# Attention over 23104 keys: four score banks, scores in a row, and maximum jobs on a ring of three PSUM banks

## The reference

```python
# x: (16, 100, 256), ctx: (16, 1444, 256); H = 16 heads of 16
def xattn(x, cond):                       # x is layer-normalised before
    q = (x @ Wq + bq) * hd ** -0.5        # all 1600 queries see all 23104 keys
    k, v = split(cond @ Wkv + bkv)
    q, k = fq_sym(q, axis=-1), fq_sym(k, axis=-1)      # to 8 bits and back, per row and head
    v = fq_sym(v, axis=2)                              # per column, over all keys
    attn = softmax(q @ k.T)                            # per head
    attn = fq_unsigned(attn, axis=-1)     # steps of max(attn) / 255 along the keys
    return (attn @ v) @ Wp + bp
x = x + xattn(layernorm(x), ctx)
x = x + ffn(layernorm(x))                 # 8 experts, two of them weighted, low-rank corrections
```

## Time and profile before

| | us |
|---|---|
| median of 3 runs | 8433.32 (8431.86 to 8435.04) |
| the profiled execution | 8431.64 |
| its span in the trace | 8429.8 |
| granted TensorE clock, mean | 0.976 |
| busy: PE, DVE, ACT, POOL | 8040.4, 6627.4, 5391.9, 5189.8 |
| the reductions of the jobs, L1316 | 5686.0 in 5017 |
| the exponentials, L1202 | 4978.3 in 11520 |

### The profile page before, as it was taken

How to read it: one execution, slowest core, us unless ns; L and a number is a source line. 1 busy time by engine, 2 the same in 40 slices (tenths; PEclk the granted TensorE clock), 3 DMA queues, 4 the chain that set the end, 5 groups by cost and what they waited for, 6 DMA issues and landing times. The chain is left out here.

```text
span 8429.8 us, 176589 instructions
## 1 busy us (share of the span) xinstructions
PE 8040.4 (95%) x60394; PEld 2517.5 (30%) x60394; DVE 6627.4 (79%) x6516; ACT 5391.9 (64%) x12186; POOL 5189.8 (62%) x3571
## 2 busy tenths in 40 slices
PE   7957999999999999999999999999999999999688
PEld 4512222222222222222222222222222222222343
DVE  8985888888888888888888888888888888884566
ACT  2314777777777777777777777777777777777333
POOL 5765666666666666666666666666666666666356
PEclk9968999999999999999999999999999999999789
DMA  5663020202020201111110202020202020110000
GB/s 162 209 215 87 25 37 23 39 19 43 18 44 14 46 16 39 23 38 23 32 30 25 38 25 37 23 39 19 43 18 44 14 47 16 39 21 22 9 4 4
DMA packets 305513, 351.63 MB, mean 42 GB/s; under 512 B 66003, under 2 KB 286879, under 8 KB 295903
## 3 DMA queue, kind: packets, MB, share of 16 engines
q1 hardware_dynamic: 304788, 342.27, 17.5%
q10 hardware_dynamic: 42, 0.00, 0.0%
HBM read 263.57 MB, written 78.41 MB: 41 GB/s over the span
## 5 line engine op out<-in xcount | busy, mean ns | idle before, releaser
L1316 DVE TENSOR_REDUCE mpart<-psum 128x1 f32<-128x978 f32 (+1 forms) x5017 | 5686.0, 1172 | 1300.4 <-PE psum L1444 1202.0
L1202 ACT ACTIVATE y<-psum 128x400 f32<-128x400 f32 x11520 | 4978.3, 506 | 2013.1 <-PE psum L1532 2001.7
L1119 POOL TENSOR_SCALAR xh<-y 128x1600 f16<-128x1600 f32 x2880 | 4397.8, 1527 | 2699.7 <-PE psum L1512 1775.0
L1532 PE MATMUL psum<-QT,K 99*128 99x400 bf16 x11520 | 3107.3, 339 | 50.5 <-ACT y L1202 48.9
L1502 PE MATMUL psum<-y,ones 128*17 128x400 f32 x23040 | 2526.6, 505 | 0.0
L1532 PEld LDWEIGHTS psum<-QT,K 99*128 99x128 bf16 x11520 | 834.5, 97 | 2491.5 <-ACT y L1202 1972.2
L1444 PE MATMUL psum<-K,QS 48*128 48x489 bf16 x8334 | 1440.4, 379 | 88.0 <-DVE mpart L1316 34.4
L1512 PE MATMUL psum<-xh,vwin 128*16 128x400 f16 x11520 | 1015.5, 334 | 12.0 <-DMA vwin<-v_int 11.3
L1444 PEld LDWEIGHTS psum<-K,QS 48*128 48x128 bf16 x8334 | 362.7, 93 | 1038.6 <-issue 860.1
L1502 PEld LDWEIGHTS psum<-y,ones 128*17 128x17 f32 x23040 | 401.4, 95 | 723.0 <-issue 722.5
L1512 PEld LDWEIGHTS psum<-xh,vwin 128*16 128x16 f16 x11520 | 321.1, 90 | 631.4 <-issue 488.9
(11 more groups left out here) (187 smaller groups left out, 2490.1 us busy)
## 6 DMA issues: line engine op xcount, KB each, us to landing
K<-kT_parts SPq DMA_DIRECT2D x288, 240.0 KB, 8.4
vwin<-v_int SPq DMA_DIRECT2D x579, 80.0 KB, 1.9
K1X<-kT_parts SPq DMA_DIRECT2D x760, 45.8 KB
kT_parts<-part SPq DMA_DIRECT2D x135, 256.0 KB, 2.8
src<-in_ctx_dram SPq DMA_DIRECT2D x46, 512.0 KB, 4.2
v_float<-kv SPq DMA_DIRECT2D x45, 512.0 KB, 4.7
vin<-v_float SPq DMA_DIRECT2D x9, 2560.0 KB, 15.3
K<-kT_parts SPq DMA_DIRECT2D x32, 450.9 KB
```

The lines of the kernel that those rows point to most:

```text
L1119: pool.tensor_scalar(xh[:, g % YR, :, :], y[:, g % YR, :, :], INT_STEP, 0.0, ALU.mult, ALU.add)\
L1202: act.activation(y[:, s % YR, j, :], s2_bank(tiles_before(h, b, c) + GT * s + j), ACT.Exp).then_inc(exp_done, 1)
L1316: dve.tensor_reduce(mpart[:, t, column], buf[:, :, 0:CHALF], AX.XY, ALU.max).then_inc(s1_free, 1)
L1532: pe.matmul(s2_bank(T + t), K3[0:MROW, c * REGION + t * P:c * REGION + (t + 1) * P], queries, start=True, stop=True).then_inc(s2_ready, 1)
```

## The change

The eight PSUM banks are divided anew: three (0 to 2) for maximum jobs and four (3 to 6) for scores; ACC stays bank 7. Slots now count banks, not jobs: slot n lies in bank n % 3, and a job takes two slots. Each of its two matmuls raises s1_ready by one; the job waits until both of its banks are free (s1_free >= at + n + 2, with 3 given at the start). VectorE reduces each bank by itself into its own column of mpart, which has 48 columns a tile in place of 24. `maxima` and `turn_out` take three slots in place of two. SPLIT and LATE are gone: all four scores of a group are issued in a row, and then all of its jobs. JOBS_AT is as before, and so is the order of sums and values. SyncE's thresholds are rewritten in the new count.

```diff
-S2_RING = 3
+S2_RING = 4
+S1_RING = 3
-SPLIT = ((1, 4, 8, 12, 14), (1, 4, 8, 12, 14), (2, 5, 9, 14))
-LATE = ((), (), (12,))
-SLOT_AT = (0, N_JOBS[0] + 2, N_JOBS[0] + 2 + N_JOBS[1])
-SLOTS_BLOCK = sum(N_JOBS) + 4
-PRO_SLOTS = 4 * CHUNKS + 2 + LEAD
+SLOT_AT = (0, 2 * N_JOBS[0] + S1_RING, 2 * N_JOBS[0] + S1_RING + 2 * N_JOBS[1])
+SLOTS_BLOCK = 2 * sum(N_JOBS) + 2 * S1_RING
+FIRST_MAX = 8 * CHUNKS
+PRO_SLOTS = FIRST_MAX + S1_RING + 2 * LEAD
-            mpart = sb("mpart", [P, PT + 1, CHUNKS], F32)
+            mpart = sb("mpart", [P, PT + 1, 2 * CHUNKS], F32)
-        def s1_buf(n):
-            return psum[:, 2 * (n % 2):2 * (n % 2) + 2, :]
+        def s1_bank(n):
+            return psum[:, n % S1_RING, :]
-            return psum[:, 4 + j % S2_RING, 0:QB]
+            return psum[:, S1_RING + j % S2_RING, 0:QB]
...
-            after_job(4 * CHUNKS - 1)
+            after_job(FIRST_MAX - 1)
...
                 act.wait_ge(mt_copied, turn + 1)
-                act.sem_inc(s1_free, 2)
+                act.sem_inc(s1_free, S1_RING)
...
         @block.vector
-            def job(t, column, at, n, buf):
-
-                dve.wait_ge(s1_ready, at + n + 1)
-                dve.tensor_reduce(mpart[:, t, column], buf[:, :, 0:CHALF], AX.XY, ALU.max).then_inc(s1_free, 1)
+            def job(t, chunk, at, n, bank):
+
+                for k in range(2):
+                    dve.wait_ge(s1_ready, at + n + k + 1)
+                    dve.tensor_reduce(mpart[:, t, ds(2 * chunk + k, 1)], bank(n + k)[:, 0:CHALF], AX.X, ALU.max)\
+                        .then_inc(s1_free, 1)
...
         @block.tensor
-            def job(tile, keys, at, n, buf):
-
-                pe.wait_ge(s1_free, at + n + 1)
+            def job(tile, keys, at, n, bank):
+
+                pe.wait_ge(s1_free, at + n + 2)
                 for k in range(2):
                     top, end = HALVES[k]
-                    last = pe.matmul(buf[:, k, 0:CHALF], tile[top:end, :], keys[top:end, :], start=True, stop=True)
-                last.then_inc(s1_ready, 1)
+                    pe.matmul(bank(n + k)[:, 0:CHALF], tile[top:end, :], keys[top:end, :], start=True, stop=True)\
+                        .then_inc(s1_ready, 1)
...
                     if c == BODY_C - 1 and s == TURN_AT and B < LASTB:
-                        maxima(B + 1, at, done, job_buf(c, done))
-                        extra = 2
-                    score_tile(s, 0)
-                    score_tile(s, 1)
-                    if s not in LATE[c]:
-                        next_jobs(1 if s in SPLIT[c] else JOBS_AT[c][s])
-                    score_tile(s, 2)
-                    score_tile(s, 3)
-                    if s in SPLIT[c] or s in LATE[c]:
-                        next_jobs(1)
+                        maxima(B + 1, at, 2 * done, job_bank(c, 2 * done))
+                        extra = S1_RING
+                    for j in range(GT):
+                        score_tile(s, j)
+                    next_jobs(JOBS_AT[c][s])
```

More of the change, by code:

```diff
@@ L596, in pe_after @@
             pe.wait_ge(fw_in, FW)
-            pe.wait_ge(s1_free, 2 + S1_END + 2)
+            pe.wait_ge(s1_free, S1_RING + S1_END + S1_RING)
             for c in range(DC):
@@ L935, in block @@
                         if q < 2 and not finish:
[L936 removed]
+                            after_job(at + 2 * EXTRAS[q] + 1)
                             sp.sem_inc(sp_passed, 1)
@@ L957, in block @@
                     if turn == 2:
-                        after_job(at + N_JOBS[c] - 1 + (2 if c != 1 else 0))
+                        after_job(at + 2 * N_JOBS[c] - 1 + (S1_RING if c != 1 else 0))
                         sp.sem_inc(sp_passed, 1)
@@ L1340, in _ @@
                 for t in range(PT + 1):
[L1341 to L1346, removed]
+                    job(t, chunk, 0, 2 * ((PT + 1) * chunk + t), s1_bank)
+            maxima(0, 0, FIRST_MAX)
+            for i in range(LEAD):
+                job(i % PT, i // PT, 0, FIRST_MAX + S1_RING + 2 * i, s1_bank)
             def outputs(B, at, n):
-                dve.wait_ge(s1_ready, at + n + 2)
-                view = job_buf(0, n)[0:SEQ, 0, 0:32 * BLOCKS].rearrange("p (s k) -> p s k", k=32)
+                dve.wait_ge(s1_ready, at + n + S1_RING)
+                view = job_bank(0, n)[0:SEQ, 0:32 * BLOCKS].rearrange("p (s k) -> p s k", k=32)
                 dve.reciprocal(rsum[:], view[:, :, HD]).then_inc(rsum_done, 1)
@@ L1363, in body @@
                     if c == BODY_C - 1 and s == TURN_AT:
-                        n += 2
+                        n += S1_RING
                     for _ in range(JOBS_AT[c][s]):
                         t, chunk, _ = job_of(c, done)
-                        column = ds(2 * (BODY_C * (B % BLOCKS) + c) + chunk, 1) if t == PT else slice(chunk, chunk + 1)
-                        job(t, column, at, n, job_buf(c, n))
-                        n += 1
+                        place = 2 * (BODY_C * (B % BLOCKS) + c) + chunk if t == PT else chunk
+                        job(t, place, at, n, lambda u: job_bank(c, u))
+                        n += 2
                         done += 1
@@ L1463, in _ @@
             pe.wait_ge(rest0, STEPS)
-            pe.sem_inc(s1_free, 2)
+            pe.sem_inc(s1_free, S1_RING)
             pe.sem_inc(exp_done, S2_RING)
@@ L1478, in _ @@
                 for t in range(PT + 1):
[L1479 to L1481 removed]
+                    job(tile_of(t, False), key_window(K1, chunk), 0, 2 * ((PT + 1) * chunk + t), s1_bank)
+            maxima(0, 0, FIRST_MAX, s1_bank(FIRST_MAX))
             pe.wait_ge(ql_in, 32)
[L1483 to L1485 removed]
+            for i in range(LEAD):
+                job(tile_of(i % PT, True), key_window(K1, i // PT), 0, FIRST_MAX + S1_RING + 2 * i, s1_bank)
             pe.wait_ge(ones_ready, 2)
@@ L1551, in next_jobs @@
                                 pe.wait_ge(k1_in[piece_of(chunk)], 32 * ((B + (2 if lead else 1)) // BLOCKS + 1))
-                        job(tile_of(t, lead), keys, at, done + extra, job_buf(c, done + extra))
+                        job(tile_of(t, lead), keys, at, 2 * done + extra, lambda u: job_bank(c, u))
                         done += 1
@@ L1591, in body @@
                     if c == 0 and s == EPI_SLOT:
-                        turn_out(block_of(h, b), at, done)
-                        extra = 2
+                        turn_out(block_of(h, b), at, 2 * done)
+                        extra = S1_RING
             def head_start(h):
@@ L1612, in _ @@
                 value_group(body_of(H, 0, 0), g)
-            turn_out(BLOCKS * H, S1_END - 2, 2)
+            turn_out(BLOCKS * H, S1_END - S1_RING, S1_RING)
             pe_after(pe)
```

41 lines of the change are left out of this document (21 added, 20 removed).

## The result

The changed kernel takes 9894.5 us (median of 4, 9891.0 to 9896.6) against 8433.9 before, a ratio of 1.173 (95% interval 1.171 to 1.175). Forecast: 9780, range 9,620 to 10,040. Its profiled execution has a span of 9894.8 us, 1465 more than before.

What follows compares the result with a forecast made beforehand. The prediction took TensorE's in-order work, 95% of the span, as the bound. From 8431.6 us, +1370 for 63 blocks with jobs (+21.75 each) and -23 for the last block gave 9779, stated as 9780 us, range 9,620 to 10,040.

Steps and rivals of the forecast that it cites:

- The stall: At next_jobs(2), a pair's second job waits for VectorE's first bank reduction: 0.94 us per two-job group, bounds 0.83 to 1.26.
- Rival A: At next_jobs(2), the second job does not wait and only score switches count: faster, 7820 us; 4 in 100.
- Four banks for scores: Four scores in a row, 0.78 us up to the first job, no wait for ScalarE; one-job groups 2.06 us (-0.21).
- The last block: Its groups without jobs go from 2.27 to 1.75 us: 45 x -0.52 = -23 us.
- The prologue: 103 jobs at 1.36 us each, 28 us later, hidden before SP's last store of V: no cost.
- The once-per-block terms: Wait for yx, chain of maxima and job after turn_out: zero together, bounds -1 and +1 us a block.
- Rival B: PE's clock falls to 1.2 GHz in the loop: near 15,100 us, or 10,700 in a third of it; 3 in 100.
- if the clock leaves 1.00: A sign that the forecast is wrong: it expected PE's granted clock to stay at 1.00 in the loop.
- The row that I argued from: From 8000 to 8020 us PE, busy 14.4 of 20 us, kept clock 1.00; cited against a clock fall.
- The sum: Whole kernel: +21.75 us a block, +1370 us over 63 blocks with jobs, and -23 us in the last block.
- The range: 9,620 to 10,040 us: stall between 0.87 and 1.05 gives -146 and +229 us, once-per-block terms +-63.

Runs made afterwards that it cites:

- The longer reduction: The changed kernel with an extra 96-element reduction ahead of each bank's reduction on VectorE: 10,269.7 us (1.217 of the kernel before).
- the second job's move: The changed kernel with a group's second job issued behind its values instead of behind its first job: 8526.5 us (1.011 of the kernel before).
- the other split of the banks: The changed kernel with four single banks for jobs and three for scores: 9309.5 us (1.104 of the kernel before).
- Written out: The changed kernel with VectorE's loop over blocks written out in full, without branch, with constant addresses and wait values: 9759.5 us (1.157 of the kernel before).
- bank by bank: The kernel before, VectorE reducing a job's two banks by two instructions: 8580.7 us (1.018); with VectorE's loop written out 8480.1 us (1.006).
- two smaller repairs: The changed kernel, second job behind the values, plus VectorE's loop written out and one last-body job moved from group 10 to 12: 8210.7 us (0.974).

## Why the prediction was right, and where it was short

**The stall.** Right in its place (next_jobs(2), the second job), its releaser and its size: 1.14 from job to job (1.15 forecast), 3.20 a group (3.21). The longer reduction shows that it is VectorE's time, the second job's move that it is the distance of the pair, the other split of the banks that it is the ring. Rival A (no stall) fell with that, and with it the idea that fewer switches decide: four scores in a row did save 0.21 in one-job groups, 0.31 in split ones, but 0.94 was lost in 33 of 45 groups.

**Four banks for scores.** Right: no wait for ScalarE in ordinary groups. The last block, where the four scores run without jobs, took 79.8 us for its first 44 groups against 101.9: -22, forecast -23; its median group takes 1.75, as forecast.

**The prologue.** Right: a job each 1.35 us (1.36), the last started at 657.2, well before SP's last store of the values, and the loop's first full score came at 683.1 against 682.2: hidden.

**The once-per-block terms.** This is the step that failed in size: "I set these at zero together". With VectorE's loop they hold another 1.10 us a block (133.80 - 132.70), 0.62 of it in the first group, where I had only a short wait for yx, and 0.43 in groups 3 and 18: 68 us over 62 blocks. I never priced VectorE's loop over a stream twice as long, nor the registers' columns, though the kernel before shows those: VectorE starts 0.63 us after group 3's K1X job there. Without that term the block's change is 132.70 - 111.16 = 21.5, forecast 21.75.

**The clock.** Rival B was given 3 in 100 as a fall that holds over the loop or a third of it; what happened is B in small, and one of the forecast's own signs of being wrong ("if the clock leaves 1.00") came true. The granted clock fell to 0.50 in 25 of the 62 blocks: (135.03 - 133.80) x 62 = 76 us. 10 of the 28 stretches begin in groups 0 and 1, behind an idle time of 1.35 to 1.63 us in front of the first group's second job. Written out, the loop has no such idle time and no such stretch, though each pair still stalls; bank by bank, with the late start and without the pairs' stall, 17 stretches follow the late start, and none with the loop written out. So these come with the late VectorE, not with the pairs alone. The other 18 begin in group 7, where PE has idled no longer than at any other pair, 0.76 us; written out, the loop has the same 0.76 there and no stretch. Why the clock fell there stays open.

The row that I argued from, 14.4 of 20 us busy at full clock, is right on a mean, but its window ends just before the granted clock falls in that same kernel. PE stood idle there for 4.55 us, took up work at 8020.45, and the clock was at 0.50 by 8021:

```profile
8020.45 2.48 PE L666 MATMUL psum<-act_c,a2T 128*16 128x400 f32 x16 [4.55 <-DVE act_c L586]
```
```profile
8021.00:8027.00 6.00, 4.97 (x19) 2.33 (x12) 0.00 (x0) 0.84 (x1) 1.28 (x2) 0.50 0.00 0
```

The Trainium skill ("TensorE: Matmul & The Clock Gate", The two states you'll see) puts an idle array at half rate. These two lines agree with it; in the changed kernel the clock fell with PE idle for at most 1.63 us at a time.

**The sum.** Forecast +1347 us, measured +1461. 68 and 76 are 144, more than the 114 missing. The first block, with a slow start either way, took 10 us more than before where 22 had been counted, and the pieces were 0.2 us a block high, 13 us; that leaves some 5 us. With VectorE's loop written out the kernel takes 9759.5, 20 below the forecast.

**The range.** That the result lies in it is partly luck. The stall was right to 0.01 us, and the +-63 us for the once-per-block terms would alone have ended at 9843, below the 9894.5 measured; the 229 us set aside for a longer stall took in an effect that had not been priced. Nor do the range's ends follow from its two parts: added, these give 9,571 to 10,072, not 9,620 to 10,040. The result lies inside either.

## What to carry to other kernels

Count a ring in what one burst of the producer needs: two jobs of two banks in a row need four banks, and with three the in-order engine pays the whole way out and back through the consumer (0.43 + 0.66 + 0.06 us here) in front of everything queued behind. If a bank can't be had, put other work of that length between the two (with two smaller repairs that turned 9894 into 8211). And when a change doubles an engine's instructions inside a loop, price the loop's turn too.

## What the runs showed of the hardware

- VectorE's first reduction of a block starts 0.42 us after its job where its loop holds 78 reductions a turn. With 156 it was 1.03 in the changed kernel, 1.87 with reductions bank by bank, 2.00 with the second job apart and 0.64 with four banks for jobs (medians); with the loop written out it was 0.41 to 0.42 in every kernel. The packets of the instruction queue q14 change with it: on the profile's page 223 before, 534 in the changed kernel, 304 with its loop written out. By their times in the trace, five more come in each of the 62 blocks (510 against 200), and one of them about 0.2 us after every block's first score, where the kernel before has none that recurs. That part of the doubled stream is fetched again in each turn, and that VectorE waits for it, is the likeliest reading; no row says so, and why the delay differs between kernels is open.
- A VectorE operation on four columns with both inputs in SBUF, 0.16 us by itself, took 1.49 when a GpSimd rounding of 1.52 us had started 0.04 before it, and 1.40 when one had started 0.14 before it; each time both ended within 0.02 us. Reductions out of PSUM beside the same rounding kept their 0.66.
- The granted clock can fall in a loop that is busy 80% of the time: 28 stretches in the changed kernel, none behind the first block with the same pairs and VectorE's loop written out. After 1.95 us of idle in front of one job (in the kernel with the second job apart) the next group ran at the low clock.
- Back to back, reductions of 489 columns out of PSUM start 0.577 apart at a duration of 0.657, those of 978 columns 1.083 apart at 1.17: neighbours overlap by 0.08 to 0.09, so splitting a reduction in two costs 0.07 us, not its whole fixed part of 0.15.
